# Mamba scan on one core: delta*u*B of three state steps made on GpSimd, their decays put in PSUM

## The reference, cut to what matters

```
delta = softplus(dt part of (u @ xproj) @ dt_w + dt_b);  Bm, Cm = the other columns of u @ xproj
dA  = exp(delta * A)                      # per channel d and state n
dBu = delta * Bm * u
h   = dA_t * h + dBu_t                    # step by step over the tokens
y_t = sum over n of h * C_t;   y = (y + u * D) * silu(res);   out = y @ out_w, then a layer norm
```

## Time and profile before

| | |
|---|---|
| median of 3 runs | 21086.46 us (21080.1 to 21098.46) |
| the profiled execution's own time | 21098.81 us |
| its span | 21097.0 us |
| mean granted TensorE clock | 0.789 |
| VectorE busy | 19421.3 us (92% of the span) |
| GpSimd busy | 15394.4 us (73%) |
| TensorE matmul busy | 14907.7 us (71%) |
| ScalarE busy | 11474.3 us (54%) |
| first to last scan | 1623.2 to 17128.0 us |

### The profile page before, as it was taken

The page is one execution under the profiler, slowest core; times in us unless marked ns, Lnnn a source line. Parts: engine busy times, 40 slices in busy tenths (PEclk is TensorE's granted clock), DMA queues, the critical chain, the costliest instruction groups (busy, mean ns, idle before and its releaser), DMA issues. The chain is left out here.

```text
span 21097.0 us, 183109 instructions
## 1 busy us (share of the span) xinstructions
PE 14907.7 (71%) x47074; PEld 5387.9 (26%) x47074; DVE 19421.3 (92%) x12666; ACT 11474.3 (54%) x12716; POOL 15394.4 (73%) x6584
## 2 busy tenths in 40 slices
PE   4876666666666666666666666666666668888885
PEld 2331222222222222222222222222222224444444
DVE  5778999999999999999999999999999978888886
ACT  1115555555555555555555555555555546666663
POOL 3766777777777777777777777777777758888881
PEclk8887777777777777777777777777777779999997
DMA  3224444444444444444444444444444421111113
GB/s 117 95 90 112 111 114 116 111 113 116 114 109 116 115 112 114 115 112 112 114 117 110 114 116 110 114 116 114 109 116 114 111 63 30 30 30 30 30 26 132
DMA packets 574458, 2089.44 MB, mean 99 GB/s; under 512 B 70785, under 2 KB 88051, under 8 KB 550067
## 3 DMA queue, kind: packets, MB, share of 16 engines
q1 hardware_dynamic: 569122, 2081.45, 39.6%
q10 hardware_dynamic: 5265, 7.14, 0.1%
HBM read 856.39 MB, written 158.18 MB: 48 GB/s over the span
## 5 line engine op out<-in xcount | busy, mean ns | idle before, releaser
L1287 POOL TENSOR_TENSOR prod<-h,c_bc 128x1024 f32<-128x1024 f32 x4096 | 9571.1, 2350 | 4069.1 <-PE py L992 3088.1
L1246 DVE TENSOR_TENSOR_SCAN h<-da,state,px 128x1024 f32<-128x1024 f32 x4096 | 9613.4, 2347 | 193.2 <-DVE px L1239 24.6
L1133 ACT ACTIVATE da<-d_bc,a_neg 128x1024 f32<-128x1024 f32 x4096 | 4666.6, 1145 | 4670.2 <-DVE h L1246 4644.1
L1239 DVE TENSOR_TENSOR px<-px,du_bc 128x1024 f32<-128x1024 f32 x4096 | 5046.0, 1232 | 359.6 <-PE px L925 141.2
L925 PE MATMUL px<-cf,bsel 32*128 32x512 f32 x4096 | 3113.4, 899 | 3199.0 <-DVE h L1246 3198.9
L992 PE MATMUL py<-prod,ysel 128*32 128x512 f32 x16384 | 2725.9, 798 | 1560.0 <-POOL prod L1287 1560.0
L1874 POOL TENSOR_TENSOR acc<-acc,ta 128x1024 f32<-128x1024 f32 (+1 forms) x1040 | 2424.7, 2339 | 499.7 <-DVE acc L1774 370.1
L925 PEld LDWEIGHTS px<-cf,bsel 32*128 32x128 f32 x4096 | 957.5, 257 | 4989.4 <-DVE h L1246 4037.7
L1774 DVE SCALAR_TENSOR_TENSOR p_c<-zb,w_dw,p_c 128x1024 f32<-128x1024 f32 (+1 forms) x1560 | 1987.3, 1274 | 42.3 <-PE p_c L1546 9.8
L992 PEld LDWEIGHTS py<-prod,ysel 128*32 128x32 f32 x16384 | 511.2, 132 | 3808.6 <-POOL prod L1287 2800.9
L1673 ACT ACTIVATE ta<-zb,w_dw 128x1024 f32<-128x1024 f32 (+1 forms) x1040 | 1168.5, 1128 | 297.1 <-POOL acc L1874 275.5
(11 more groups left out here) (219 smaller groups left out, 18319.6 us busy)
## 6 DMA issues: line engine op xcount, KB each, us to landing
d_bc<-delta SPq DMA_DIRECT2D x1024, 512.0 KB, 8.1
du_bc<-du SPq DMA_DIRECT2D x1024, 512.0 KB, 7.7
c_bc<-c_rows_dram SPq DMA_DIRECT2D x1024, 512.0 KB, 4.0
hx<-x_dram SPq DMA_DIRECT2D x252, 256.5 KB, 4.8
st_x<-in_x_dram SPq DMA_DIRECT2D x32, 1024.0 KB, 4.8
ax<-in_x_dram SPq DMA_DIRECT2D x64, 512.0 KB, 3.4
xr<-x_dram SPq DMA_DIRECT2D x64, 512.0 KB, 6.0
x_dram<-xo SPq DMA_DIRECT2D x64, 512.0 KB, 5.3
```

What stands on the lines that cost most here:

```text
L1133: nc.scalar.activation(da[n % 4][:, :], d_bc[:, n % J, :], ACT.Exp, scale=a_neg[t.l][:, n:n + 1]).then_inc(da_done, 1)
L1239: nc.vector.tensor_tensor(out=x[:, :], in0=px[q % 2][:, :], in1=du_bc[:, j, :], op=ALU.mult).then_inc(m1_done, 1)
L1246: nc.vector.tensor_tensor_scan(h[:, n % 8, :], da[n % 4][:, :], x[:, :], state[:, 2 * t.l + t.b, n:n + 1], ALU.mult, ALU.add).then_inc(sca ...
L1287: nc.gpsimd.tensor_tensor(out=prod[j][:, :], in0=h[:, n % 8, :], in1=c_bc[q % 2][:, :], op=ALU.mult).then_inc(m2_done, 1)
```

## The change

- Steps 8, 9 and 10 (POOL_X) get x = delta*u*B from GpSimd, in three new SBUF tiles xs, from du_bc and a new broadcast tile b_bc, which SP fills from DRAM (the rows of B now go there beside those of C). GpSimd makes them right after products 0, 2 and 3 of the same task. Their decays are written by ScalarE into the px tile that is free at that time. VectorE only scans in these steps.
- B of quarter 2 is needed from step 11 on and is spread after scan 9; that of quarter 3 after scan 10. The px tiles' roles now go by task parity. The decays are issued in the order DECAYS, and the four da tiles turn over the 13 other steps.
- The two 512-column halves of a spread of B now read different groups of 32 rows (cf and bsel are held twice for each parity).
- GpSimd's product is in place in h: the scan writes columns 8 to 1031 of a tile 1032 wide, and the product goes to columns 0 to 1023. prod is gone, add_y reads h. GpSimd no longer waits for add_y; VectorE does at scans 0, 4, 8 and 12, for the sum of the products of two quarters back.
- TensorE's and ScalarE's programs are reordered; the gate is one step later; front_dl and front_du one earlier, back_zn one later.

Core of the diff:

```diff
+    POOL_X = (8, 9, 10)
+    NX = len(POOL_X)
+    NM = N - NX
+    PAD = 8
...
-        h = sb("h", [128, 8, T])
-        prod = [sb(f"prod{i}", [128, T]) for i in range(4)]
+        h = sb("h", [128, 8, T + PAD])
+        b_bc = sb("b_bc", [128, T])
+        xs = [sb(f"xs{i}", [128, T]) for i in range(NX)]
...
-        GATE_AT, STATS_AT = 2, 6
-        OUT_AT, DL_AT, DU_AT, ZN_AT = 0, 8, 9, 12
+        GATE_AT, STATS_AT = 3, 6
+        OUT_AT, DL_AT, DU_AT, ZN_AT = 0, 7, 8, 13
+        POOL_X_AT = {0: 0, 2: 1, 3: 2}
+        DECAYS = (0, 1, 2, 3, 4, 5, 6, 7, 11, 12, 8, 13, 9, 10, 14, 15)
+        TILED = tuple(n for n in range(N) if n not in POOL_X)
...
+            def spread_b(t):
...
+                if t.from_(1):
+                    eng.wait_ge(xs_done, t.nth(NX - 1, NX) - NX)
+                eng.wait_ge(c_out, stored)
+                first = POOL_X[0] // 4 * 4
+                eng.dma_start(b_bc[:, :], dram["c_rows"][t.par, first:first + 4, :].partition_broadcast(32)).then_inc(b_in, 16)
...
             def spread_first(t):
-                spread_delta(t, 0)
-                spread_delta(t, 1)
-                spread_delta(t, 2)
+                for j in range(J - 1):
+                    spread_delta(t, j)
+                spread_b(t)
+                spread_delta(t, J - 1)
                 spread_du(t, 0)
                 spread_c(t, 0)
-                spread_delta(t, 3)
...
             def spread_b(t, q):
                 if q == 0:
                     pe.wait_ge(cf_done, t.nth())
-                if q or t.from_(1):
-                    pe.wait_ge(scanned, t.nth(4 * q - 2, N))
-                rows = slice(32 * t.par, 32 * t.par + 32)
-                halves(px[q % 2], bsel[rows, q, :], cf[rows, :]).then_inc(b_ps, 1)
+                    if t.from_(1):
+                        pe.wait_ge(scanned, t.nth(14, N) - N)
+                else:
+                    pe.wait_ge(scanned, t.nth((None, 2, 9, 10)[q], N))
+                for i in range(2):
+                    cut = slice(i * HALF, (i + 1) * HALF)
+                    rows = slice(64 * t.par + 32 * i, 64 * t.par + 32 * i + 32)
+                    last = nc.tensor.matmul(px[(t.par + q + q // 2) % 2][:, cut], bsel[rows, q, :], cf[rows, cut], start=True, stop=True)
+                last.then_inc(b_ps, 1)
...
             def main(t, before, after, done):
+                if after:
+                    front_u(after, t)
                 if before:
                     add_y(before, 3)
+                spread_b(t, 1)
                 if after:
-                    front_u(after, t)
-                spread_b(t, 1)
+                    front_res(after)
                 skip(t)
                 if after:
-                    front_res(after)
+                    front_bc(after)
                 add_y(t, 0)
                 if after:
-                    front_bc(after)
-                spread_b(t, 2)
-                if after:
                     front_dt(after)
-                add_y(t, 1)
                 if before:
                     back_z(before, t, after)
+                spread_b(t, 2)
+                add_y(t, 1)
                 spread_b(t, 3)
...
             def decay(t, n):
...
+                if n in POOL_X:
+                    out = px[(t.par + n) % 2]
+                    act.wait_ge(scanned, t.nth(n - 2, N))
...
             def main(t, before, after, done):
...
+                decay(t, 6)
+                if after:
+                    front_silu(after)
+                decay(t, 7)
+                decay(t, 11)
+                keep_state(t, 0)
+                if after:
+                    front_bc(after)
+                decay(t, 12)
+                if after:
+                    front_abs(after)
+                decay(t, 8)
+                if after:
+                    front_exp(after)
+                decay(t, 13)
+                decay(t, 9)
+                if after:
+                    front_ln(after)
+                decay(t, 10)
+                decay(t, 14)
+                if before:
+                    back_z(before)
+                keep_state(t, 1)
+                decay(t, 15)
...
+                    if n in POOL_X:
+                        a, x = px[(t.par + n) % 2], xs[POOL_X.index(n)]
+                        dve.wait_ge(xs_done, t.nth(POOL_X.index(n), NX))
...
+                    dve.wait_ge(da_done, t.nth(DECAYS.index(n), N))
+                    if j == 0 and (n >= 8 or t.from_(1)):
+                        dve.wait_ge(y_sum, t.nth(q, Q) - 2)
+                        dve.wait_ge(st_done, t.nth(q, Q) - 2)
+                    nc.vector.tensor_tensor_scan(h[:, n % 8, PAD:T + PAD], a[:, :], x[:, :], state[:, 2 * t.l + t.b, n:n + 1],
...
+            def front_x(t, i):
+                n = POOL_X[i]
+                if i == 0:
+                    pool.wait_ge(b_in, 16 * t.nth())
+                pool.wait_ge(du_in[n % J], 16 * t.nth())
+                if t.from_(1):
+                    pool.wait_ge(scanned, t.nth(n, N) - N)
+                nc.gpsimd.tensor_tensor(out=xs[i][:, :], in0=du_bc[:, n % J, :], in1=b_bc[:, :], op=ALU.mult).then_inc(xs_done, 1)
...
-                        if q or before:
-                            pool.wait_ge(y_sum, t.nth(q, Q) - 1)
-                    nc.gpsimd.tensor_tensor(out=prod[j][:, :], in0=h[:, n % 8, :], in1=c_bc[q % 2][:, :],
+                    nc.gpsimd.tensor_tensor(out=h[:, n % 8, 0:T], in0=h[:, n % 8, PAD:T + PAD], in1=c_bc[q % 2][:, :],
                                             op=ALU.mult).then_inc(m2_done, 1)
+                    if n in POOL_X_AT:
+                        front_x(t, POOL_X_AT[n])
```

More of the change, by code:

```diff
@@ L699, in mamba_layer @@
         w_res = [sb(f"w_res{l}", [64, 128]) for l in range(2)]
-        w_bc = [sb(f"w_bc{l}", [128, 32]) for l in range(2)]
+        w_bc = [sb(f"w_bc{l}", [128, 64]) for l in range(2)]
         w_dt = [sb(f"w_dt{l}", [128, 128]) for l in range(2)]
@@ L1130, in decay @@
                     act.wait_ge(d_in[n], 16 * t.nth())
-                if n >= 4 or t.from_(1):
-                    act.wait_ge(scanned, t.nth(n, N) - 4)
-                nc.scalar.activation(da[n % 4][:, :], d_bc[:, n % J, :], ACT.Exp,
+                if n in POOL_X:
+                    out = px[(t.par + n) % 2]
+                    act.wait_ge(scanned, t.nth(n - 2, N))
+                else:
+                    out = da_of(t, n)
+                    at = TILED.index(n) - 4
+                    if at >= 0:
+                        act.wait_ge(scanned, t.nth(TILED[at], N))
+                    elif t.from_(1):
+                        act.wait_ge(scanned, t.nth(TILED[at], N) - N)
+                nc.scalar.activation(out[:, :], d_bc[:, n % J, :], ACT.Exp,
                                      scale=a_neg[t.l][:, n:n + 1]).then_inc(da_done, 1)
@@ L1143, in main @@
                     act.preload_act_table_set("natural_log_exp_and_others")
[L1144 to L1152, removed]
-                    if after:
[L1154 to L1158, removed]
-                            front_bc(after)
-                        if n == SOFT_AT:
-                            front_soft(after)
-                    if before:
-                        if n == Z_AT:
-                            back_z(before)
-                        if n == LN_AT:
-                            back_ln(before)
-                        if n == RSTD_AT:
-                            back_rstd(before)
-                        if n == NORM_AT:
-                            back_norm(before)
@@ new lines, in main @@
+                decay(t, 3)
+                if after and after.l == 0:
+                    norm_hx(after)
+                decay(t, 4)
+                if before:
+                    keep_state(before, 3)
+                decay(t, 5)
+                decay(t, 6)
[7 more added lines that the diff above has]
+                decay(t, 12)
@@ new lines, in main @@
+                if after:
[9 more added lines that the diff above has]
+                decay(t, 14)
+                if before:
+                    back_z(before)
+                keep_state(t, 1)
+                decay(t, 15)
+                if before:
+                    back_ln(before)
+                    back_rstd(before)
@@ L1172, in _ @@
+                for n in range(3):
+                    if after:
+                        decay(after, n)
+                    if n == 0:
+                        keep_state(t, 2)
+                if before:
+                    back_norm(before)
             norm_hx(FIRST)
@@ L1175, in _ @@
             front_soft(FIRST)
-            for n in range(AHEAD):
+            for n in range(3):
                 decay(FIRST, n)
@@ L1229, in main @@
             def main(t, before, after, done):
+                near, far = px[t.par], px[1 - t.par]
+                dbu = {**{n: (near, far) for n in range(3)}, 3: (near, near), **{n: (far, near) for n in range(4, 7)}, 7: (far, far),
```

(24 more changed lines are left out.)

51 lines of the change are left out of this document (25 added, 26 removed).

## The result

The changed kernel takes 21311.2 us (median of 4 runs, 21309.5 to 21318.3) against 21091.0 of the kernel before (median of 4 runs): a ratio of 1.0105, 95% interval 1.0088 to 1.0123. It is slower by 220 us, where 20341 was forecast, in a range up to 20850. The profiled execution took 21309.7 us (before 21098.8).

A forecast was written before the change was run, and what follows sets the result against it. VectorE bounds the scan stage, busy 97%. Per task -3.81 (multiplications, gaps) - 0.55 (old B wait) + 1.2 (new B wait) + 0.2 (ScalarE chain) = -2.96 us, x 256 = -758 us: 20341 us, range 19970 to 20850.

The forecast's parts named there:

- Decay 6 ends at 12.1 ... done at 17.6: ScalarE: SiLU part of 7.44 us, less skip's 1.99, follows decay 6 and ends at 17.6 us of the task.
- +0.2 us: ScalarE's chain to decays 8 to 10: fits with 0.4 us to spare, misses by about 1.3 in one of four.
- Three gaps of some 0.035 us: VectorE, steps 8 to 10: these gaps go with the three multiplications, -3.81 us per task together.
- The wait for B: VectorE waiting on TensorE's spreads of B, at steps 11 and 12: +1.2 us per task; the old 0.55 goes.
- Half clock at the spread for step 11: TensorE idles from about 31 to 35.15 us, so this spread runs at half clock in two tasks of three.
- The overlap of the halves: TensorE's spread of B from two row groups: 0.68 x 3.78 = 2.6 us at half clock, bounds 1.9 and 3.78.
- Rival B: TensorE's two halves of a spread of B do not overlap: -1.3 us per task, 20766 us; chance 0.13.
- the three multiplications: VectorE, steps 8, 9 and 10: 3 x 1.232 us per task removed, leaving multiplications x3328 at 1232 ns.
- rival C: Loop through ln, front_dl and GpSimd binds, 52.4 to 55.9 us; with 1.5 us lost, 20725 us; chance 0.12.
- the price of the product in place: GpSimd's product written in place in h costs the same as the others, about 2350 ns.
- D: GpSimd becomes the bound: in-place products at 3350 ns, 68.3 us per task, 23080 us; chance 0.06.
- The 0.07 or so for slower: Chance that the whole kernel gets slower; faster was given 0.91.

The follow-up runs named there:

- e1: Changed kernel with the gate back at step 2, nothing else: 20443.5 us, ratio to the kernel before 0.9698.
- e2: Changed kernel, gate left at step 3, but SiLU to u no longer waits for the gate: 20446.0 us, ratio to the kernel before 0.9699.
- e4: Changed kernel with VectorE waiting for the decay first and for its own multiplication last: 21317.8 us, ratio to the kernel before 1.0113.
- e7: e1 and e4 together, gate at step 2 and VectorE's own wait last: 20432.8 us, ratio to the kernel before 0.9690.
- e8: e7 with both spreads of B ahead of add_y(1) on TensorE: 20429.5 us, ratio to the kernel before 0.9687.
- e5: e1 with both halves of a spread of B read from one group of 32 rows again: 21317.0 us, ratio to the kernel before 1.0108.
- e3: Changed kernel with ScalarE's order only, decays 8, 9, 10 ahead of abs, exp, ln: 20742.9 us, ratio to the kernel before 0.9839.
- e9: e7 and e3 together, adding ScalarE's new order of decays: 20172.1 us, ratio to the kernel before 0.9562.
- e11: e7 with TensorE multiplying back_z three times in place of once, same result: 20177.5 us, ratio to the kernel before 0.9567.

## Why the prediction was wrong, point by point

- **The step that failed** is in the working of ScalarE: "Decay 6 ends at 12.1 ... done at 17.6". It let SiLU start right behind decay 6. In fact SiLU also waits for the gate, which in the same working ends at 15.8: the same prediction writes "gate (1.24) now after step 3" and counts only its place in VectorE's time, not who waits for it. From that start its own chain (decay 6 to the end of decay 8, 17.0 us) would have had decay 8 at 32.8, 2.4 us late against S7; the trace has 2.7 in the mean, and 0.67 for decay 9. e1 and e2 remove it in two independent ways, by 868 and 865 us.
- The term "+0.2 us" for ScalarE's chain measured 3.34 us. Its durations were right (17.7 us from the table load to the end of decay 8 in the changed kernel, where 5.5 for SiLU and 11.5 behind it make 17.0), its start was not.
- "Three gaps of some 0.035 us" and a step of 3.65 us missed that the scans' gap would change: 0.98 us per task. By e4 and the trace the cause is the value computed between two waits. It was in reach of the diff: m1_done and da_done counted the same before, and do not after. Taking the gaps away gave nothing back by itself, neither in the changed kernel (e4) nor with the gate at step 2 (e7).
- The wait for B: +1.2 was forecast, of which 0.86 (221 us) came, at step 12 alone and for the reason given, the place behind add_y(1) (e8 removes it). Two of its parts were off. Half clock at the spread for step 11 was counted in two tasks of three; it came in nearly all (2.08 us in the median). The overlap of the halves was undersized: 0.68 of the time in line was taken, 0.55 to 0.57 measured, and the spread for step 12 took 1.13 us, at full clock. The Trainium skill (TensorEngine Tiling (Array Packing), Key Properties) says that different tiles load weights and multiply in parallel. Read as one half, that was nearer here than the row of L1520. Rival B, no overlap, was priced 425 us above the forecast; e5 shows 874 above e1: VectorE's wait for px grows by 702 us and that for decays by 207. That the late first B pushes TensorE's queue, and with it the decays, was not tried by itself.
- Right: the three multiplications (974 us off VectorE with their count as said), the price of the product in place, x ready in time, no wait of GpSimd for py, the DMA queue's room, and in part rival C, whose chain through ln and front_dl shows next (e3, e9). With the gate at step 2 the kernel is at 20443 us, 102 above the forecast: gaps +0.98 us per task, B 0.83 in place of 1.2, decays 0.08 in place of 0.2. That the rest comes so near is in part luck, since the gaps and the size of the B term were wrong in opposite directions.
- Of the rivals, D, to which most of the slower side was given, did not happen: products took 2356 ns. The slower side came by a wait that no rival named. The 0.07 or so for slower was too low for a change that reorders the programs of four engines: the slack found in the chain was 0.4 us, and each wait that I had not looked up could use it.

## What to carry to other kernels

When a piece is moved by a step, look up every wait on the semaphore that it raises, on all engines and for the tasks two back, before its own time is counted; a wait that shows no idle time in the trace may only tie with another. What is short of time should not stand in an engine's order behind a chain whose length depends on other engines: placing the three decays first (with the gate back and the waits turned) was worth 261 us on top. An engine at its bound is not sped up by cutting its gaps while a longer loop closes through the others.

## What the runs showed of the hardware that was not expected

- The two halves of a spread, matmuls of 32-row operands from different row groups into different banks, overlapped almost wholly: 1.13 to 1.18 us against 1.98 at full clock, 2.08 against 3.77 at half.
- More matmuls made the kernel faster (e11, 255 us), because TensorE idled 1.4 in place of 4.4 us ahead of the work that VectorE waits for, and did that work at full clock.
- Kernels with different waits came out with the same time per task: 61.44 us in the changed kernel, e4 and e5; 58.03 in e1, e2, e7 and e8. The gaps saved in e4 and e7 reappeared as waits for B and for decays, with more of TensorE's work at half clock in the stretches shown. Why just these two values is left open.
- In a loop, a semaphore value that must be computed between an engine's own wait and its next instruction cost 0.09 us each time on VectorE (gaps of 0.12 against 0.04).
- The exponential written to PSUM took 1111 ns against 1144 to SBUF, and a scan with its decay in PSUM took what any scan takes.
